# A gated cross-attention and top-2 mixture-of-experts layer on one core: choice steps with scratch in PSUM, conversions dealt out anew, register loads inside block 7, no filler products before block 0

## The reference

```python
x = x + tanh(g_xattn) * xattn(layernorm(x), ctx, Wq, bq, Wk, bk)   # softmax over 256 keys
x = x + tanh(g_ffn) * ffn(layernorm(x), ...)

# ffn
logits = gelu(x @ rw1) @ rw2
wgt, idx = top_k(softmax(logits), 2)
for e in range(8):
    Ye = gelu(x @ w1[e] + b1[e]) @ w2[e] + b2[e]
    Ce = gelu(b1[e]) @ w2[e] + b2[e]
    for k in range(2):
        mask = idx[..., k] == e
        out = out + any(mask) * wgt[..., k:k+1] * where(mask[..., None], Ye, Ce)
```

## Time and profile before

| | us |
|---|---|
| median of 3 runs | 200.49 |
| lowest, highest | 199.53, 202.08 |
| the profiled execution | 201.76 |
| its span, first to last instruction | 199.92 (shown as 199.9) |

### The profile page before, as it was taken

One profiled execution on the slowest core, in us unless ns is written; L12 is line 12 of the kernel. 1 busy time (PEld: TensorE's weight loads), 2 busy tenths in 40 slices (PEclk: granted clock), 3 DMA queues, 4 the chain that ended last, 5 costly groups with the idle time before them and its releaser, 6 DMA issues.

```text
span 199.9 us, 5212 instructions
## 1 busy us (share of the span) xinstructions
PE 161.8 (81%) x1722; PEld 137.8 (69%) x1723; DVE 133.5 (67%) x294; ACT 102.4 (51%) x256; POOL 115.6 (58%) x173
## 2 busy tenths in 40 slices
PE   6899995948169999599498599699499999998930
PEld 2457983814059999499397599598499999886610
DVE  2666589788635779989996266945566677464185
ACT  0588977727828999469487144243044433440000
POOL 0029999999868999678886414454155444203100
PEclk9999999996967999889999999999999999999955
DMA  6899354598377655945509435556166666430495
GB/s 178 252 387 331 123 152 169 181 279 271 118 211 256 232 175 201 320 147 177 197 21 387 139 113 225 216 228 234 46 241 249 247 232 219 192 113 33 125 325 200
DMA packets 21028, 40.69 MB, mean 204 GB/s; under 512 B 2741, under 2 KB 12047, under 8 KB 21010
## 3 DMA queue, kind: packets, MB, share of 16 engines
q1 hardware_dynamic: 17680, 34.54, 49.6%
q0 software_dynamic: 1872, 4.73, 7.4%
q10 hardware_dynamic: 1458, 1.19, 1.8%
HBM read 23.66 MB, written 4.60 MB: 141 GB/s over the span
## 4 chain that ended last, share of the span: by engine, by line
PE 45%; POOL 17%; DVE 13%; DMA 11%; issue 7%; SPq 3%; DVEq 1%; ACT 1%; POOLq 0%; ACTq 0%
POOL w_lo L401 11%; PE bank L1299 8%; PE bank L1301 7%; PE bank L1300 7%; PE bank L1310 7%; PE bank L1312 7%; PE bank L1311 7%; DMA stage<-in_L_ffn_w 4%; POOL w_hi L408 3%; DMA stage<-y_table 3%; DVE lnT L952 2%; DMA x_table<-probT 2%; DMA probT<-x_table,gidx 2%; DVE en L923 2%; DMA y_table<-lnx,ycol 1%
## 5 line engine op out<-in xcount | busy, mean ns | idle before, releaser
L654 ACT ACTIVATE bank<-bank,b1T 128x128 f32<-128x128 f32 x152 | 42.3, 342 | 57.7 <-PE bank L1301 57.7
L1310 PE MATMUL bank<-w_hi,cf 128*128 (+1 forms) x152 | 41.8, 275 | 9.8 <-DVE lnT L952 9.8
L401 POOL TENSOR_TENSOR w_lo<-stage,w_hi 128x256 bf16<-128x256 f32 x64 | 48.2, 787 | 0.7
L1311 PE MATMUL bank<-w_lo,cf 128*128 (+1 forms) x152 | 41.8, 275 | 0.8 <-issue 0.8
L1312 PE MATMUL bank<-w_hi,lnT 128*128 (+1 forms) x152 | 41.9, 276 | 0.0
L1300 PE MATMUL bank<-cfT,stage 128*128 128x128 bf16 x176 | 34.0, 219 | 0.0
L1299 PE MATMUL bank<-cfT,stage 128*128 128x128 f16 x176 | 34.0, 219 | 0.0
L1301 PE MATMUL bank<-cfT,stage 128*128 128x128 f16 x176 | 34.0, 219 | 0.0
L418 POOL TENSOR_TENSOR held<-cst 128x1 f32<-128x1 f32 x31 | 6.8, 218 | 39.0 <-DVE lnx L965 37.7
L952 DVE TENSOR_TENSOR lnT<-bank,cf 128x512 bf16<-128x512 f32 x38 | 26.1, 688 | 4.0 <-ACT cf L661 3.3
L519 ACT ACTIVATE w_hi<-stage 128x1024 f16<-128x1024 f32 x24 | 25.0, 1049 | 7.1 <-POOL cfT L414 5.6
(11 more groups left out here) (195 smaller groups left out, 340.7 us busy)
## 6 DMA issues: line engine op xcount, KB each, us to landing
stage<-in_L_ffn_w SPq DMA_DIRECT2D x32, 512.0 KB, 4.6
stage<-w_hi SPq DMA_DIRECT2D x12, 512.0 KB, 3.0
stage<-w_lo SPq DMA_DIRECT2D x12, 512.0 KB, 3.7
stage<-y_table SPq DMA_DIRECT2D x8, 256.0 KB, 4.7
xs<-in_x SPq DMA_DIRECT2D x2, 512.0 KB, 7.9
out<-stage SPq DMA_DIRECT2D x4, 256.0 KB, 2.7
cf<-in_ctx SPq DMA_DIRECT2D x1, 512.0 KB, 5.4
x_table<-cfT ACTq DMA_DIRECT2D x2, 256.0 KB, 4.2
```

The source lines that it names most:

```text
L401: last = nc.gpsimd.tensor_tensor(out=w_lo[:, q, n:n + PIECE], in0=stage[:, q % RING, n:n + PIECE], in1=w_hi[:, q, n:n + PIECE], op=ALU.sub ...
L654: last = nc.scalar.activation(h, h, ACT.Gelu, bias=bias)
L1310: mm(o, h_hi[:, u, c, :], w2_hi[:, ex, 1, c, :], start=(c == 0), stop=False)
L1311: mm(o, h_hi[:, u, c, :], w2_lo[:, ex, 1, c, :], start=False, stop=False)
```

## The change

- **Scratch in PSUM.** The choice steps of iterations 1 to 4 take their scratch from `aside[u]`, the upper half of bank 2 or 3 (`same` from bank 5), and each group begins with a copy of its SBUF input into that scratch. `en` is worked out in `rest_of_starts`, without the addition of P, which the comparisons take up as a constant. `scatter_rows` reads the codes in PSUM.
- **VectorE's order.** The choice steps of iteration i stand before the conversions `behind`; conversions 11, 12 and 13 move: scatter rows, counts and bias copy come first, then 11, tokens of block 0, 12, tokens of block 1, 13.
- **Who converts.** VectorE's low parts: 18 and 25 are added, 20 is taken out. GpSimd's high parts: 20 in place of 9. ScalarE makes the high part of 9; those from 16 on stand behind its gelus (L654), one behind each half block, without 20 and 27.
- **GpSimd's and ScalarE's order at the front.** GpSimd does its four `token_low` right behind quarter 5, then lows of 8, 9, 10. ScalarE does `token_high` earlier, and `send` with quarters 8 to 11 between.
- **SyncE.** It is quarter 16, not 17, that waits for the first gather.
- **TensorE.** The filler products before the choice (6), before the one-hot products (4) and behind them (9) are gone; the single ones ahead of each four remain. The register loads stand inside block 7, behind column groups 1, 3 and 5.

```diff
...
 sprod = scratch[:, 6 * TE:8 * TE].rearrange("p (k t e) -> p k t e", k=TOPK, t=T)
-rest = lnx_flat[:, 4 * D:4 * D + 8 * TE]
-ge = rest[:, 0:TE].rearrange("p (a b) -> p a b", a=N_EXP)
-ltc = rest[:, TE:TE + N_EXP * (N_EXP + 1)].rearrange("p (a b) -> p a b", a=N_EXP)
-slotb = rest[:, 3 * TE:4 * TE].rearrange("p (t e) -> p t e", t=T)
-rprod = rest[:, 4 * TE:6 * TE].rearrange("p (k t e) -> p k t e", k=TOPK, t=T)
-rslot, blk_i = [rest[:, 6 * TE + n * TOPK * T:6 * TE + (n + 1) * TOPK * T].bitcast(I32) for n in range(2)]
+aside = [bank[2 + u][:, 2 * P:4 * P] for u in range(2)]
...
-DVE_QUARTERS = (6, 7, 11, 12, 13, 15, 17, 19, 20, 22, 23, 26, 28, 29, 30, 31)
-POOL_HIGHS = (0, 1, 2, 3, 4, 5, 9, 27)
+DVE_QUARTERS = (6, 7, 11, 12, 13, 15, 17, 18, 19, 22, 23, 25, 26, 28, 29, 30, 31)
+POOL_HIGHS = (0, 1, 2, 3, 4, 5, 20, 27)
...
             sp.wait_ge(*low_done(q - RING))
-        if q == 17:
+        if q == 16:
             sp.wait_ge(gathered[0], 16)
...
     own(0, 6)
-    lows(8, 9)
-    token_low(0)
-    own(9, 10)
-    token_low(1)
-    token_low(2)
-    token_low(3)
-    lows(10, 11)
+    for b in range(4):
+        token_low(b)
+    lows(8, 11)
     wait(index_ready, 1)
...
     refill(7, 1, 3, 16)
-    lows(18, 19)
+    own(20, 21)
     put(1, 1)
...
     lows(24, 25)
+    put(3, 1)
     wait(index_ready, 2)
     refill(NS, 0, 4, 32)
-    put(3, 1)
-    lows(25, 26)
     own(27, 28)
...
     high(7, 8)
+    token_high(0)
+    xnT_copy(1)
     second_deviation(2)
-    xnT_copy(1)
-    high(8, 9)
+    token_high(1)
     second_deviation(3)
...
     router_gelu(1)
-    token_high(0)
     xnT_copy(3)
-    token_high(1)
+    token_high(2)
     router_gelu(2)
-    token_high(2)
+    token_high(3)
     router_gelu(3)
-    token_high(3)
+    high(8, 9)
     send(0)
+    high(9, 10)
+    send(1)
     high(10, 11)
-    send(1)
+    send(2)
+    send(3)
     high(11, 12)
-    send(2)
-    high(12, 13)
-    send(3)
     act.wait_ge(choice_ready, 1)
...
     nc.scalar.activation(warm[:, 2:3], tg[:, 0:1], ACT.Gelu)
-    high(13, 17)
+    high(12, 16)
...
+    later = [q for q in range(16, QUARTERS) if q not in POOL_HIGHS]
     for i in range(NS):
...
             hidden_high(i, i % 2, half)
-            q = 17 + 2 * i + half
-            if q >= 27:
-                q += 1
-            high(q, min(q + 1, QUARTERS))
+            if 2 * i + half < len(later):
+                high(later[2 * i + half], later[2 * i + half] + 1)
...
-    def scatter_rows(a, b):
-        c = code[:, a:b]
-        nc.vector.tensor_scalar(yt1[:, a:b], c, 0.0, float(SKIP), ALU.is_equal, ALU.mult)
+    def scatter_rows(a, b, c, spare):
+        nc.vector.tensor_scalar(spare, c, 0.0, float(SKIP), ALU.is_equal, ALU.mult)
         step(nc.vector.tensor_scalar(yt2[:, a:b], c, 0.0, float(SECOND), ALU.is_lt, ALU.mult))
-        step(nc.vector.tensor_tensor(out=yt1[:, a:b], in0=yt1[:, a:b], in1=yt2[:, a:b], op=ALU.add))
-        step(nc.vector.tensor_tensor(out=yidx[:, a:b], in0=yt1[:, a:b], in1=gidx[:, a:b], op=ALU.add))
+        step(nc.vector.tensor_tensor(out=spare, in0=spare, in1=yt2[:, a:b], op=ALU.add))
+        step(nc.vector.tensor_tensor(out=yidx[:, a:b], in0=spare, in1=gidx[:, a:b], op=ALU.add))
...
-    def rest_of_starts():
-        step(nc.vector.tensor_tensor(out=ge, in0=nexp[:, :].unsqueeze(2).broadcast_to(ee),
+    def rest_of_starts(spare):
+        many = spare[:, 0:N_EXP]
+        more = spare[:, N_EXP:2 * N_EXP + 1]
+        ge = spare[:, TE:2 * TE].rearrange("p (a b) -> p a b", a=N_EXP)
+        ltc = spare[:, 2 * TE:2 * TE + N_EXP * (N_EXP + 1)].rearrange("p (a b) -> p a b", a=N_EXP)
+        nc.vector.memset(more[:, N_EXP:N_EXP + 1], 1.0)
+        step(nc.vector.tensor_copy(many, nexp[:, :]))
+        step(nc.vector.tensor_tensor(out=ge, in0=many.unsqueeze(2).broadcast_to(ee),
                                      in1=thr.unsqueeze(1).broadcast_to(ee), op=ALU.is_ge))
         step(nc.vector.tensor_reduce(out=more[:, 0:N_EXP], in_=ge, axis=X, op=ALU.add))
-        step(nc.vector.tensor_tensor(out=ltc, in0=lt, in1=more[:, :].unsqueeze(1).broadcast_to(ec),
-                                     op=ALU.mult))
+        step(nc.vector.tensor_tensor(out=ltc, in0=lt, in1=more.unsqueeze(1).broadcast_to(ec), op=ALU.mult))
         step(nc.vector.tensor_reduce(out=st_[:, :], in_=ltc, axis=X, op=ALU.add))
-
-    def rest_of_blocks():
+        step(nc.vector.scalar_tensor_tensor(out=en[:, :], in0=more[:, 0:N_EXP], scalar=float(P), in1=st_[:, :],
+                                            op0=ALU.mult, op1=ALU.add))
+
+    def rest_of_blocks(spare):
+        starts = spare[:, 0:N_EXP]
+        rslot, blk_i = [spare[:, TOPK * T * n:TOPK * T * (n + 1)].bitcast(I32) for n in (1, 2)]
+        slotb = spare[:, TE:2 * TE].rearrange("p (t e) -> p t e", t=T)
+        rprod = spare[:, 2 * TE:4 * TE].rearrange("p (k t e) -> p k t e", k=TOPK, t=T)
+        same = bank[5][:, D:D + TOPK * T * REST].rearrange("p (k n) -> p k n", n=REST)
         rank_te = rank_s[:, :].rearrange("p (t e) -> p t e", t=T)
-        step(nc.vector.tensor_tensor(out=slotb, in0=rank_te, in1=e_bc(st_[:, :]), op=ALU.add))
+        step(nc.vector.tensor_copy(starts, st_[:, :]))
+        step(nc.vector.tensor_tensor(out=slotb, in0=rank_te, in1=e_bc(starts), op=ALU.add))
         step(nc.vector.scalar_tensor_tensor(out=slotb, in0=rank_te, scalar=float(P), in1=slotb,
...
         step(nc.vector.tensor_scalar(blk_i, rslot, SLOTS - P, None, ALU.bitwise_and))
-        step(nc.vector.tensor_tensor(out=oh_rest, in0=iota_b[:, N_EXP:BLOCKS].unsqueeze(1).broadcast_to(kb),
+        step(nc.vector.tensor_tensor(out=same, in0=iota_b[:, N_EXP:BLOCKS].unsqueeze(1).broadcast_to(kb),
                                      in1=blk_i.unsqueeze(2).broadcast_to(kb), op=ALU.is_equal))
-        nc.vector.tensor_tensor(out=oh_rest, in0=oh_rest,
+        nc.vector.tensor_tensor(out=oh_rest, in0=same,
                                 in1=tokp1.rearrange("p k t -> p (k t)").unsqueeze(2).broadcast_to(kb),
...
-    def experts_of_blocks():
-        step(nc.vector.scalar_tensor_tensor(out=en[:, :], in0=more[:, 0:N_EXP], scalar=float(P), in1=st_[:, :],
-                                            op0=ALU.mult, op1=ALU.add))
-        step(nc.vector.tensor_tensor(out=en[:, :], in0=en[:, :], in1=eend, op=ALU.add))
+    def experts_of_blocks(spare):
+        ends = spare[:, 0:N_EXP]
+        found = spare[:, 2 * N_EXP:2 * N_EXP + BLOCKS]
         be = [P, BLOCKS, N_EXP]
-        step(nc.vector.tensor_tensor(out=ebge, in0=iota_b.unsqueeze(2).broadcast_to(be),
-                                     in1=en[:, :].unsqueeze(1).broadcast_to(be), op=ALU.is_ge))
-        step(nc.vector.tensor_reduce(out=ebf[:, :], in_=ebge, axis=X, op=ALU.add))
-        nc.vector.tensor_scalar(eb[:, :], ebf[:, :], float(N_EXP - 1), None, ALU.min).then_inc(eb_ready, 1)
-
-    def rest_of_indices():
+        behind_end = spare[:, TE:TE + BLOCKS * N_EXP].rearrange("p (b e) -> p b e", b=BLOCKS)
+        step(nc.vector.tensor_copy(ends, en[:, :]))
+        step(nc.vector.scalar_tensor_tensor(out=behind_end, in0=iota_b.unsqueeze(2).broadcast_to(be),
+                                            scalar=float(P), in1=ends.unsqueeze(1).broadcast_to(be),
+                                            op0=ALU.subtract, op1=ALU.is_ge))
+        step(nc.vector.tensor_reduce(out=found, in_=behind_end, axis=X, op=ALU.add))
+        nc.vector.tensor_scalar(eb[:, :], found, float(N_EXP - 1), None, ALU.min).then_inc(eb_ready, 1)
+
+    def used_counts(spare):
+        ends = spare[:, 0:N_EXP]
+        used_f = spare[:, N_EXP:N_EXP + 3]
+        whole = spare[:, 2 * N_EXP:2 * N_EXP + 3].bitcast(I32)
+        used = ((0, P + LEAST_LAST * 2 * P, 2 * P), (1, LEAST_ODD * 2 * P, 2 * P), (2, LEAST * P, P))
+        for n, least, size in used:
+            last = nc.vector.tensor_scalar(used_f[:, n:n + 1], ends[:, N_EXP - 1:N_EXP], float(least - P), None,
+                                           ALU.subtract)
+        step(last)
+        step(nc.vector.tensor_copy(whole, used_f))
+        for n, least, size in used:
+            last = nc.vector.tensor_scalar(used_i[:, n:n + 1], whole[:, n:n + 1], size.bit_length() - 1, None,
+                                           ALU.logical_shift_right)
+        last.then_inc(used_ready, 1)
+
+    def rest_of_indices(spare):
         dve.wait_ge(codes_done, 2)
...
                                             in1=c, op0=ALU.mult, op1=ALU.max))
-        scatter_rows(N_EXP, BLOCKS)
-        nc.vector.tensor_copy(held_v[:, :], eps[:, :]).then_inc(index_ready, 1)
+        scatter_rows(N_EXP, BLOCKS, c, spare[:, 0:REST])
+        nc.vector.tensor_copy(held_v[:, :], spare[:, 0:1]).then_inc(index_ready, 1)
...
         nc.vector.tensor_copy(ysb[:, y_slot(i, u), :], bank[4 + u][:, 0:D]).then_inc(y_ready, 1)
...
-    low(11)
-    low(12)
-    scatter_rows(0, N_EXP)
+    scatter_rows(0, N_EXP, first, scratch[:, 0:N_EXP])
     counts_of_choices()
...
```

(43 more changed lines are left out.)

17 lines of the change are left out of this document (removed).

## The result

| | before | after |
|---|---|---|
| median, four runs each | 200.92 | 194.34 |
| lowest, highest | 199.53, 202.08 | 192.12, 197.66 |
| the profiled execution | 201.76 | 195.22 |
| its span | 199.9 | 193.3 |

By the medians the changed kernel takes 6.6 us less, where 11.6 us were forecast. The ratio is 0.960, with a 95% interval of 0.948 to 0.972. The direction and the range held, the point was 5.4 us too low.

What follows compares the result with a forecast made beforehand. TensorE was taken as the bound, plus its waits for the first gather, VectorE's hidden_low and ahead of the pair loop. 3.0 + 6.8 + 2.4 - 0.6 = 11.6 us less gave 188.9 us from the median, range 185.3 to 195.8.

Steps and rivals of the forecast that it cites:

- Part 1: Blocks 1 to 4: choice steps with PSUM scratch end TensorE's waits for VectorE's hidden_low; gain 6.8 us, bounds 0 and 6.8.
- rival (c): Choice steps: PSUM operands don't free them from waiting for GpSimd; 195.7 us, chance 0.08.
- Part 2: Between block 7 and pair loop: register loads moved into block 7 mostly hide; gain 2.4 us, bounds 0 and 3.1.
- Part 3: Way to the first gather: GpSimd's new order sends it at 49.65, not 52.63; gain 3.0 us, bounds 0 and 3.9.
- my bound of 3.9: First gather: the best case of the front's gain, 3.9 us, if the indices set when it goes out.
- near 54.5: Sign for the front in the profile after: TensorE's block 0 starts near 54.5 us, first gather issued at 49 to 50.
- Rival (b): Front gains nothing, as weights and tables share the DMA engines and the gather lands no earlier; 191.9 us, chance 0.08.
- Part 4: Front, around the choice: removing TensorE's filler products costs nothing; price 0, bounds 0 and 0.5 us.
- Rival (d): Without filler products the clock stays at half beyond block 0; three such blocks give 205.4 us; chance 0.05.
- Part 5: Expert blocks: conversions re-placed between VectorE and GpSimd cost 0.6 us in small waits for hidden_low and weights; bounds 0 and 3.
- rival (a): Expert blocks: VectorE becomes the bound in each block; 5.1 us lost, 194.0 us, chance 0.17.
- A half clock beyond 62 us: Sign against the forecast, which expected full clock from the end of block 0 to the pair loop.

Runs made afterwards that it cites:

- the second profile of before: The kernel before, unchanged, profiled once more as the mark for what varies from run to run: 200.26 us.
- PSUM alone: The kernel before with only the choice steps' scratch moved to PSUM; order, conversions, loads and filler products as before: 197.25 us, against 199.32 before.

## Why the prediction was right or wrong

**Part 1, the choice steps: the mechanism right, the size by luck.** The steps are 0.15 to 0.43 us, and with the scratch in SBUF alone they are back to 1.67 and 2.18: rival (c) falls. The -6.81 us against -6.8 is no merit. 1.7 of it was half clock and 3.2 the add of 3.50 us, and the second profile of before had neither; against that one, block 4 to 7 gained 2.9 us. By the experiment the scratch is worth 4.6 to 5.2 us in these blocks and 1.3 to 1.8 up to the loop. My lower bound, 0 for the clock, was right, and I didn't use it for the add.

**Part 2, the register loads: the mechanism was right, the gain was not to be had.** Charged 0.7 us exposed inside block 7, measured 0. But 2.4 us of gain became +0.06, as gather 9 was not there yet; in the second profile of before it was that gather, too, which set the gap (2.5 us). The 3.09 us with no releaser were one reading of a gap with two causes nearly level: with the loads in it, it was 2.5, 2.6 and 2.7 us in three other profiles, each time ended by the gather. I never asked when the gather goes out.

**Part 3, the front: right in this profile, -4.26 against -3.0, and conditional.** I had GpSimd's work set the gather at 49.65; it was done at 48.38, with its token lows at 40.43 instead of 41.7, and the indices set it, at 49.94: the case of my bound of 3.9. Block 0's start moved by 3.36 us. Its sign for block 0, "near 54.5", didn't follow from its own sum either (56.27 less 3.0 is 53.3). And two of its 3.0 us came from counting the low part of quarter 10 at 2.55 us where the kernel before took 4.52, without saying why; that held, as the twelve pieces took 7.57 us. But the worth hangs on when the choice begins: 4.5 us with an early one, above that bound, and nearly nothing behind a late one. Rival (b) falls for early choices.

**Part 4, the filler products: right.** Price 0, measured 0 from choice to loop. Choice to indices took 8.77 us instead of 8.49, the 0.3 us of its upper working. I said that full speed would be back behind block 0, and it was, at 59.30. Rival (d) falls. The Trainium skill (TensorE: Matmul & The Clock Gate, "What's actually happening") calls the throttled state the default that activity releases. By that rule the trace agrees: 17.10 us of half clock without the products, 6.8 with them. But the time didn't follow the clock there, as other engines set the pace.

**Part 5, the re-placed conversions: the term that failed.** "I charge 0.6 us in small waits for `hidden_low` and weights; bounds 0 and 3." Measured at its place: 0.91 us for quarter 27, 2.07 us for the gather queued behind it, and 1.6 us of half clock after that: 4.6 us, beyond its own upper bound. These are the waits that kept part 2's gain away, not a second loss. The rows to see it by were named: GpSimd busy 16.36 of 17.20 us, and eight pieces that took 7.03 us, four alone 2.55. I summed GpSimd's conversions for the front only, and not for block 7. That the re-placing made these waits is not shown: they are there with PSUM alone, and smaller waits of this kind in the second profile of before. They are what a TensorE that comes earlier runs into. They belong to rival (a), "VectorE becomes the bound in each block", in another form: GpSimd, once, at the end. Its price of 5.1 us lost (194.0 us) came close to the 5.4 missing, by a sum made for another place.

**The rest is the clock.** "A half clock beyond 62 us would prove me wrong": it came at 103.70 and at 134.40. The second, behind a wait of 2.85 us in the loop, costs 1.4 us; of the fourteen profiles twelve had a stretch of half clock in the loop, and one of the two without was that from which I counted. Half clock in the router's stage goes with the 0.90 us that the choice came late; in the kernels with this front and without it the choice came at 39.2 to 39.5.
